# A two-layer graph attention kernel: its one-trip loop written out, and its opening loads and first projection in another order

## The chip, the cores and the metric

The kernel runs on one core of a Trainium2 chip. The core has five engines that each take their own stream of instructions in order: TensorE (PE, matrix products and transposes), VectorE (DVE), ScalarE (ACT), GpSimd (POOL) and SyncE (SP, which here only issues DMAs). They meet through semaphores. The metric is the device time of one launch in microseconds (us); lower is better.

## The reference

128 graphs of 128 nodes with 384 features go through two attention layers, each after a layer norm and a ReLU and with a residual. Both layers have 12 heads of 32; `adj` masks the first layer's scores and is added to the second's.

```python
h = jnp.maximum(_layernorm(x), 0.0)
q, k, v = split(h @ Wq + bq), split(h @ Wk + bk), split(h @ Wv + bv)      # layer 0
scores = einsum('bhqd,bhkd->bhqk', q, k) / sqrt(32) + beta * adj
scores = where(adj > 0, scores, -9e15)
x = x + einsum('bhqk,bhkd->bhqd', softmax(scores), v)
h = jnp.maximum(_layernorm(x), 0.0)
q, k, v = h @ Wq1.T, h @ Wk1.T, h @ Wv1.T + bv1                            # layer 1
a = softmax(einsum(q, k) * 384 ** -0.5 + adj)
x = x + einsum(a, v) @ Wo1.T + bo1
```

## The kernel before

**Units and phases.** Four graphs make a group, and a group in one layer is a *unit*; there are 64 units. A unit is normed (DVE, ACT, POOL), turned by a DMA transpose into `h`, projected on PE in ten *jobs* (0 to 5 make q and k by column blocks, 6 to 9 make the values of a graph each), and attended in twelve *chunks* of four heads (c = 0 to 11). These steps belong to different phases: a `Phase` (from line 130) attends one unit, projects the next, norms the one after that and finishes the tail of the one before. A phase has 12 slots, and every engine's code walks through slots and places within a slot and emits what is due. So the order on each engine is written by hand, in tables: `PROJ` says how many of a unit's 90 projection matmuls stand in each slot's three places, and the `..._AT` tables place the other steps.

**Products in two halves.** Every weight and every activation is split into two fp16 parts, high and low, and a product takes three matmuls (high by high, low by high, high by low). For a weight that is one ACT instruction (`high_weight`, w_hi, L658) and one DVE instruction (`low_weight`, w_lo, L766), both on a float32 copy that SP loads (`load_weight`, L457) into a buffer that is used for something else later (`staging`). `LOAD_SLOTS`, `HIGH_SLOTS` and `LOW_SLOTS` say in which slot of which of the first four phases each of the seven weights (0 to 6) is handled. Weights 0, 1 and 2 are layer 0's for q, k and v.

**q and k.** The result of a job is taken from its bank by ACT (`part_hi`, L679) and DVE (`part_lo`, L865); a bank is free for the job after next once `part_lo` is written. Three DMAs of 128 KB for each job (L483, L487) then copy the parts into `stack`, in which a head's 96 rows stand together. Scores for chunks 0, 1 and 2 wait for the stacks of jobs 0 and 1, 2 and 3, 4 and 5 (`stack_in`, one semaphore for each pair). The first job of a unit waits for all four of its DMA transposes (`h_in`, L518).

**The opening.** Phase 0 norms unit 0 and takes weights 0, 1 and 2 apart. Phase 1 projects unit 0 and norms unit 1, whose input is `x_second` (it stands in the buffer `probs_t`). The transposes of unit 0 read h_rows0, h_rows1, o_t and o_norm, in this order; so do those of unit 1. Phase 2 is the first that attends. All DMAs are issued by SP, on one queue. The two norm tables say in which slots the four graphs of a unit begin: `NORM_SLOTS_FIRST` is (0, 1, 2, 3).

**The loop.** `run_phases` (L211) writes seven phases, then a loop (`Fori`, L214) over `inside`, then twelve more. The loop's step is 24 pairs of phases and it makes one trip, so its body is all 48 phases, and the values it waits for are constants in the program as built; each engine has one jump into the body and one addition, comparison and branch at its end.

## Time and profile before

| what | us |
|---|---|
| median of three runs | 2213.1 (2212.03 to 2213.17) |
| the profiled execution, its own time | 2209.57 |
| its span, first instruction to last | 2207.8 |
| PE busy in the span | 2155.2 (98%) |
| ACT busy | 2048.4 (93%) |
| DVE busy | 1818.2 (82%) |
| POOL busy | 1511.8 (68%) |
| chain that ended last: PE's share of it | 82% |

The first line is what is to be predicted; the others come from one profiled execution. Busy time is the time in which an engine works on an instruction; what it waits for between is in the view of waits. The chain is followed back from the last instruction to whatever released each step.

### The profile page before, as it was taken

To read this page: it belongs to the slowest core of one execution; us is meant where nothing else is said; L and a number is where in the kernel's file an instruction comes from. 1 tells how busy PE (TensorE), PEld (TensorE's weight loads), DVE (VectorE), ACT (ScalarE), POOL (GpSimd) and SP (SyncE) were. 2 spreads that over 40 slices of the span, in tenths; PEclk is the share of its full clock that TensorE was granted. 3 is DMA by queue.
4 is the path that set the end of the run, shared out by engine and by line. 5 is a ranking of instruction groups with operands and counts; after the bars stand their busy time and mean duration, and the time that the engine had idled before them with its cause. 6 is when DMAs were issued, how large, how long until landed. Compare 5 with 4: busy or idle time off the path is not lost.

```text
span 2207.8 us, 69320 instructions
## 1 busy us (share of the span) xinstructions
PE 2155.2 (98%) x19968; PEld 1423.3 (64%) x19968; DVE 1818.2 (82%) x10202; ACT 2048.4 (93%) x7824; POOL 1511.8 (68%) x2407
## 2 busy tenths in 40 slices
PE   5999999999999999999999999999999999999997
PEld 2566666666666666666666666666666666666665
DVE  5888888888888888888888888888888888888787
ACT  4999999999999999999999999999999999999987
POOL 1567766767667767667676677676676776676675
PEclk9999999999999999999999999999999999999999
DMA  9886768778577787787797777776776876868852
GB/s 192 170 134 140 132 136 145 128 134 159 125 137 141 135 146 134 138 145 132 133 154 129 135 144 132 143 147 129 141 136 133 158 127 134 146 131 133 140 99 60
DMA packets 461307, 302.88 MB, mean 137 GB/s; under 512 B 228480, under 2 KB 460928, under 8 KB 460928
## 3 DMA queue, kind: packets, MB, share of 16 engines
q1 hardware_dynamic: 460928, 298.45, 73.8%
q8 instruction: 162, 2.65, 0.6%
q14 instruction: 217, 1.78, 0.4%
HBM read 71.83 MB, written 25.17 MB: 44 GB/s over the span
## 4 chain that ended last, share of the span: by engine, by line
PE 82%; ACT 6%; DVE 6%; issue 4%; DMA 1%; SPq 0%; DVEq 0%; POOL 0%; ACTq 0%
PE job_bank L999 43%; PE pt_bank L1022 13%; PE o_bank L1035 8%; PE score_bank L1012 7%; ACT probs L667 4%; PE inv_bank L1058 3%; PE post_bank L1068 2%; PE post_bank L1072 2%; PE post_bank L1069 2%; PE post_bank L1050 2%; DVE neg L787 1%; DVE part_lo L865 1%; ACT part_hi L679 1%; DVE inv_wide L857 1%; DMA x_norm<-in_x 1%
## 5 line engine op out<-in xcount | busy, mean ns | idle before, releaser
L667 ACT ACTIVATE probs<-neg,neg_max 128x128 f32<-128x128 f32 x3072 | 1189.7, 394 | 45.4 <-DVE neg_max L787 45.4
L999 PE MATMUL job_bank<-h,w_hi 128*128 128x512 f16 x2304 | 725.4, 380 | 23.1 <-DMA h<-o_norm 21.1
L667 ACT ACTIVATION_READ_ACCUMULATOR probs<-neg,neg_max 128x1 f32 x3072 | 595.0, 194 | 0.0
L692 ACT ACTIVATE probs_t<-pt_bank 128x512 f32<-128x512 f32 x768 | 450.3, 586 | 29.1 <-PE pt_bank L1022 26.4
L1022 PE MATMUL pt_bank<-ident,probs 128*128 128x128 f32 x3072 | 464.1, 274 | 11.5 <-ACT probs_t L692 11.1
L999 PE MATMUL job_bank<-h,w_lo 128*128 128x512 f16 x1152 | 438.3, 380 | 0.0
L1022 PEld LDWEIGHTS pt_bank<-ident,probs 128*128 128x128 f32 x3072 | 366.1, 141 | 96.1 <-issue 16.9
L999 PE MATMUL job_bank<-w_hi,h 128*128 128x384 f16 x1536 | 411.9, 326 | 0.2 <-DVE part_lo L865 0.2
L599 POOL TENSOR_TENSOR pair_sum<-neg 128x256 f32<-128x256 f32 x384 | 281.1, 732 | 189.2 <-DVE neg_max L787 174.6
L787 DVE CUSTOM_DVE_ANT_0 neg<-score_bank,adj 128x128 f32<-128x128 f32 x1536 | 352.5, 285 | 44.2 <-issue 40.6
L787 DVE CUSTOM_DVE_ANT_0 neg<-score_bank,bias 128x128 f32<-128x128 f32 x1536 | 354.3, 287 | 15.2 <-issue 15.0
L999 PEld LDWEIGHTS job_bank<-h,w_hi 128*128 128x128 f16 x2304 | 222.0, 98 | 211.3 <-issue 32.0
L1012 PEld LDWEIGHTS score_bank<-stack 96*128 96x128 f16 x3072 | 232.5, 97 | 126.4 <-DVE neg_max L787 6.3
L1012 PE MATMUL score_bank<-stack 96*128 96x128 f16 x3072 | 299.2, 219 | 5.3 <-DMA stack<-part_lo 5.3
L787 DVE DVE_READ_ACCUMULATOR2_ANT neg_max<- 128x1 f32 x3072 | 253.4, 82 | 0.1
L999 PE MATMUL job_bank<-w_lo,h 128*128 128x384 f16 x768 | 250.6, 326 | 0.0
L568 POOL TENSOR_TENSOR rstd<-shift_var,minus_half 128x1 f32<-128x1 f32 x256 | 144.5, 564 | 146.3 <-DVE shift_var L825 146.3
L590 POOL TENSOR_TENSOR h_rows<-h_rows 128x384 f16<-128x384 f32 x248 | 226.8, 915 | 20.7
L618 POOL TENSOR_TENSOR x_mid<-x_res,o_rows 128x384 f32<-128x384 f32 x128 | 128.0, 1000 | 138.7 <-issue 110.3
L1035 PE MATMUL o_bank<-probs_t,v 128*32 128x128 f32 x6144 | 220.8, 277 | 0.0
L870 DVE SCALAR_TENSOR_TENSOR part_lo<-job_bank,part_hi 128x512 f16<-128x512 f32 x192 | 132.5, 690 | 97.6 <-ACT part_hi L683 95.3
L605 POOL TENSOR_TENSOR four_sum<-pair_sum 128x128 f32<-128x128 f32 x384 | 176.2, 459 | 38.6 <-POOL pair_sum L599 0.4
(75 smaller groups left out, 3511.0 us busy)
## 6 DMA issues: line engine op xcount, KB each, us to landing
stack<-part_hi SPq DMA_DIRECT2D x768, 128.0 KB, 3.7
stack<-part_lo SPq DMA_DIRECT2D x384, 128.0 KB, 4.0
x_res<-in_x SPq DMA_DIRECT2D x32, 768.0 KB, 6.0
out_x<-result_rows SPq DMA_DIRECT2D x128, 192.0 KB, 3.3
x_norm<-in_x SPq DMA_DIRECT2D x30, 768.0 KB, 6.8
adj<-in_adj SPq DMA_DIRECT2D x64, 256.0 KB, 3.7
h<-h_rows SPq DMA_TRANSPOSE x252, 4.0
x_norm<-in_x SPq DMA_DIRECT2D x4, 192.0 KB, 4.2
```

Source lines behind the costliest of these rows:

```text
L568: pool.tensor_tensor(rstd[:, b:b + 1], shift_var[:, b, 1:2], minus_half[:, :], ALU.pow).then_inc(rstd_done, 1)
L590: pool.tensor_tensor(h_rows[b % 2][:, 1, :], h_rows32[:, :], h_rows[b % 2][:, 0, :], ALU.subtract).then_inc(h_rows_ready, 1)
L599: pool.tensor_tensor(pair_sum[:, :, :], neg[c % 2][:, :, 0:NODES // 2], neg[c % 2][:, :, NODES // 2:NODES], ALU.add).then_inc(pair_sum_don ...
L605: pool.tensor_tensor(four_sum[b % 2][:, first:first + HC, :], pair_sum[:, :, 0:NODES // 4], pair_sum[:, :, NODES // 4:NODES // 2], ALU.add ...
L667: last = act.activation(probs[c % 2][:, h, :], neg[c % 2][:, h, :], ACT.Exp, bias=neg_max[:, b, first + h:first + h + 1], scale=-1.0, accu ...
L692: act.activation(probs_t[b % 2][:, first:first + HC, :].rearrange("p h q -> p (h q)"), pt_bank[:, :], ACT.Copy).then_inc(probs_t_ready, 1)
L787: last = dve.tensor_tensor_reduce(out=neg[c % 2][:, h, :], in0=score_bank[c % 2][:, P * h:P * (h + 1)], in1=bias, scale=(-1.0 / SCORE0 if ...
L870: last = dve.scalar_tensor_tensor(part_lo[t][:, c, :], job_bank[j % 2][:, :], scale, part_hi[t][:, c, :], ALU.mult, ALU.subtract)
L999: last = pe.matmul(to, stationary, moving, start=(m == 0), stop=(m == MATMULS - 1))
L1012: last = pe.matmul(score_bank[c % 2][:, P * h:P * (h + 1)], q[0:3 * HEAD, c % KC, h, nodes], k[0:3 * HEAD, c % KC, h, nodes], start=True, ...
L1022: last = pe.transpose(pt_bank[:, P * h:P * (h + 1)], probs[c % 2][:, h, :], ident[:, :])
L1035: last = pe.matmul(o_bank[d:d + HEAD, f:f + P], v32[u.parity][:, b, HEAD * h:HEAD * (h + 1)], probs_t[b % 2][:, h, :], start=True, stop=True)
```

## The change

Six things are changed. (1) `loop_unit`, `TURN` and the `Fori` go; Python writes out all phases, and the tests for whether a number is known go with them. (2) SP loads all four graphs of unit 0 ahead of weight 0. (3) The load of weight 2 (the values' weight) moves from the end of the opening loads to behind the transposes of unit 0, and its two halves are made in phase 1; ACT makes the halves of weights 0 and 1 behind the norm of unit 0. (4) In phase 1 the projection has its 90 matmuls from slot 0 on, nine in each of ten slots, and the norm of unit 1 begins a slot later. (5) The loads of `x_second`, of the first `adj0`, of `x_norm` for unit 2 and of `x_res` for unit 0 all stand ahead of phase 1 on SP; before, the last two stood behind it. (6) The first stack of unit 0 waits for two weights, and that of unit 1 for three.

```diff
-PROJ_FIRST = ((0, 0, 0),) * 4 + ((4, 4, 3),) * 6 + ((4, 4, 4),) * 2
+PROJ_FIRST = ((3, 3, 3),) * 10 + ((0, 0, 0),) * 2
...
+NORM_SLOTS_SECOND = (1, 2, 3, 4)
...
-LOAD_SLOTS = ({}, {}, {0: 3, 3: 4, 6: 5, 9: 6}, {})
-HIGH_SLOTS = ({2: 0, 3: 1, 5: 2}, {}, {3: 3, 6: 4, 9: 5}, {0: 6})
-LOW_SLOTS = ({4: 0, 6: 1, 8: 2}, {}, {4: 3, 7: 4, 10: 5}, {1: 6})
+LOAD_SLOTS = ({7: 2}, {}, {0: 3, 3: 4, 6: 5, 9: 6}, {})
+HIGH_SLOTS = ({4: 0, 5: 1}, {1: 2}, {3: 3, 6: 4, 9: 5}, {0: 6})
+LOW_SLOTS = ({6: 0, 7: 1}, {2: 2}, {4: 3, 7: 4, 10: 5}, {1: 6})
...
     for p in before()[first:]:
         phase(p)
-    with eng.Fori(FIRST_LOOP, LAST_LOOP + 2 - TURN, TURN) as i:
-        for k in range(TURN):
-            for p in inside(i, k):
-                phase(p)
+    for i in range(FIRST_LOOP, LAST_LOOP + 1):
+        for p in inside(i):
+            phase(p)
...
-            load_first(0)
-            load_first(1)
...
+            for b in range(GROUP):
+                load_first(b)
             load_weight(0)
-            load_first(2)
-            load_first(3)
             load_weight(1)
...
-            load_weight(2)
...
-                if j == 0 and isinstance(u.n, int) and u.n == 0:
-
-                    sp.wait_ge(w_lo_ready, 3)
+                if j == 0 and u.n < 2:
+
+                    sp.wait_ge(w_lo_ready, 2 + u.n)
...
-                    if p.weights == 0 and s == 5:
-                        sp.dma_start(x_second, x_groups[1]).then_inc(x_second_in, 16)
...
             phase(before()[0])
+            sp.dma_start(x_second, x_groups[1]).then_inc(x_second_in, 16)
             sp.dma_start(adj0[:, :, :], adj_groups[0]).then_inc(adj0_in, 16)
+            sp.wait_ge(centred_ready, GROUP)
+            sp.dma_start(x_norm[:, :, :], x_groups[2]).then_inc(x_norm_in, 16)
+            sp.dma_start(x_res[:, :, :], x_groups[0]).then_inc(x_res_in, 16)
             phase(before()[1])
-            sp.dma_start(x_res[:, :, :], x_groups[0]).then_inc(x_res_in, 16)
```

Three places of the order show it. The first is SP's queue in phase 0, from the last of the small loads on: before,

```order
L470 DMA bo_rows<-in_L1_gnn_bo 128x384
L457 DMA stack01<-in_L0_gnn_Wv 128x3x384
L518 DMA_TRANSPOSE h0<-h_rows0 128x6x128 [waits h_rows_ready]
L518 DMA_TRANSPOSE h0<-h_rows1 128x6x128 [waits h_rows_ready]
L518 DMA_TRANSPOSE h0<-o_t 128x6x128 [waits h_rows_ready]
L541 DMA probs_t1<-in_x 128x4x384
L518 DMA_TRANSPOSE h0<-o_norm 128x6x128 [waits h_rows_ready]
L546 DMA adj0<-in_adj 128x4x128
```

and in the changed kernel:

```order
L453 DMA bo_rows<-in_L1_gnn_bo 128x384
L500 DMA_TRANSPOSE h0<-h_rows0 128x6x128 [waits h_rows_ready]
L500 DMA_TRANSPOSE h0<-h_rows1 128x6x128 [waits h_rows_ready]
L500 DMA_TRANSPOSE h0<-o_t 128x6x128 [waits h_rows_ready]
L500 DMA_TRANSPOSE h0<-o_norm 128x6x128 [waits h_rows_ready]
L440 DMA stack01<-in_L0_gnn_Wv 128x3x384
L522 DMA probs_t1<-in_x 128x4x384
L523 DMA adj0<-in_adj 128x4x128
L525 DMA x_norm<-in_x 128x4x384 [waits centred_ready]
L526 DMA x_res<-in_x 128x4x384
L465 DMA stack00<-part_hi0 32x4x512 [waits part_hi_ready,w_lo_ready]
```

The four transposes of unit 0 have nothing large right ahead of them now, and five loads stand between them and the first stack. The second place is the end of phase 1 on SP (`stack00` and `stack10` are unit 0's q and k, h1 is unit 1's): before,

```order
L483 DMA stack10<-part_hi1 32x4x512 [waits part_hi_ready]
L483 DMA stack10<-part_hi1 32x4x512
L487 DMA stack10<-part_lo1 32x4x512 [waits part_lo_ready]
L536 DMA x_norm<-in_x 128x4x384 [waits centred_ready]
L548 DMA x_res<-in_x 128x4x384
L496 DMA adj0<-in_adj 128x4x128 [waits bias_ready]
```

and now:

```order
L500 DMA_TRANSPOSE h1<-o_t 128x6x128 [waits h_rows_ready]
L465 DMA stack10<-part_hi1 32x4x512 [waits part_hi_ready]
L465 DMA stack10<-part_hi1 32x4x512
L469 DMA stack10<-part_lo1 32x4x512 [waits part_lo_ready]
L500 DMA_TRANSPOSE h1<-o_norm 128x6x128 [waits h_rows_ready]
L478 DMA adj0<-in_adj 128x4x128 [waits bias_ready]
```

The last transpose of unit 1 stood ahead of the stacks of jobs 2 to 5; now it stands behind all 18 stacks of unit 0. The third place is PE where phase 1 passes into phase 2, the same rows in both kernels but for their lines; here the changed kernel's:

```order
L991 MATMUL score_bank1<-stack10,stack00 128x128 [waits stack_in10]
L991 MATMUL score_bank1<-stack10,stack00 128x128 x3
L978 MATMUL job_bank0<-h1,w_hi0 128x512 [waits v_ready,h_in1,h_in0]
L978 MATMUL job_bank0<-h1,w_hi0 128x512
L991 MATMUL score_bank0<-stack10,stack00 128x128 [waits neg_ready,stack_in20]
L991 MATMUL score_bank0<-stack10,stack00 128x128 x3
```

Behind the scores of chunk 1 stand two matmuls of unit 1's first job, which wait for its transposes, and then the scores of chunk 2, which wait for the last stacks.

## Rows read from the trace of the kernel before

**Rows 1.** The page, part 1: busy time of each engine, share, instructions.

```profile
PE 2155.2 (98%) x19968; PEld 1423.3 (64%) x19968; DVE 1818.2 (82%) x10202; ACT 2048.4 (93%) x7824; POOL 1511.8 (68%) x2407
```

**Rows 2.** Stretches of 67.27: length, busy time of each engine, PEclk, DMA.

```profile
217.27:284.54 67.27, 67.02 (x626) 44.37 (x624) 56.33 (x319) 63.53 (x246) 47.52 (x76) 1.00 0.75 140
...
351.81:419.08 67.27, 66.67 (x623) 44.09 (x622) 55.93 (x317) 63.26 (x244) 47.82 (x76) 1.00 0.82 139
...
1831.00:1898.30 67.30, 67.07 (x626) 44.47 (x625) 56.28 (x318) 63.61 (x245) 47.61 (x77) 1.00 0.75 139
```

**Rows 3.** PE's waits in 0 to 56: for whom, total, times, longest.

```profile
PE job_bank L999 <- DMA h<-o_norm: 21.1, 1, 21.1
PE score_bank L1012 <- DMA stack<-part_lo: 5.3, 1, 5.3
```

**Rows 4.** PE's waits in 54 to 2160.

```profile
PE inv_bank L1058 <- DVE inv_wide L857: 7.3, 29, 0.6
PE pt_bank L1022 <- ACT probs_t L692: 4.0, 10, 0.7
```

**Rows 5.** Timeline of SP, 0 to 29: start, length, what it issued.

```profile
2.12 0.96 SPq L452 DMA_DIRECT2D x_norm<-in_x  x2
...
7.18 0.43 SPq L457 DMA_DIRECT2D stack<-in_L_gnn_Wv  x1
9.11 3.86 SPq L518 DMA_TRANSPOSE h<-h_rows  x2
13.08 1.84 SPq L518 DMA_TRANSPOSE h<-o_t  x1
14.97 0.57 SPq L541 DMA_DIRECT2D probs_t<-in_x  x1
15.66 1.22 SPq L518 DMA_TRANSPOSE h<-o_norm  x1
...
26.25 1.22 SPq L518 DMA_TRANSPOSE h<-o_t  x1
```

**Rows 6.** The chain of waits, 0 to 60: start, length, what.

```profile
2.12 5.77 DMA x_norm<-in_x
```

**Rows 7.** DMAs issued in 40.5 to 43: KB each, us from issue to landing.

```profile
x_norm<-in_x SPq DMA_DIRECT2D x1, 768.0 KB, 10.0
x_res<-in_x SPq DMA_DIRECT2D x1, 768.0 KB, 11.5
x_mid<-in_L_gnn_Wq SPq DMA_DIRECT2D x1, 576.0 KB, 12.6
```

**Rows 8.** The stack tiles in 27 to 49: issues, and shortest, median, longest landing.

```profile
L483 SPq DMA_DIRECT2D stack<-part_hi x12: 584/602/706, 27.6 to 39.3; - x12
...
L487 SPq DMA_DIRECT2D stack<-part_lo x6: 593/600/602, 29.0 to 40.0; - x6
...
DMA to landing us min/median/max: 3.1/5.1/8.7
```

**Rows 9.** DMAs issued in 22 to 27.

```profile
h<-o_t SPq DMA_TRANSPOSE x1, 2.7
```

**Rows 10.** Stretches of the opening: columns as in Rows 2.

```profile
21.10:26.60 5.50, 5.50 (x14) 1.87 (x15) 4.38 (x23) 4.42 (x8) 2.54 (x4) 1.00 0.30 52
26.60:43.40 16.80, 16.09 (x88) 7.95 (x86) 9.29 (x25) 5.74 (x14) 0.00 (x0) 1.00 1.07 147
43.40:48.70 5.30, 0.02 (x1) 0.00 (x0) 0.81 (x8) 1.87 (x10) 0.00 (x0) 0.86 1.13 184
48.70:53.90 5.20, 5.19 (x23) 3.58 (x24) 3.14 (x24) 1.97 (x7) 1.18 (x3) 0.50 1.08 356
...
52.60:113.40 60.80, 57.13 (x524) 36.64 (x523) 49.88 (x269) 60.05 (x222) 33.99 (x50) 0.99 0.87 171
```

**Rows 11.** Timeline of PE and ACT behind the wait for the stacks.

```profile
48.71 0.61 PE L1012 MATMUL score_bank<-stack 96*128 96x128 f16 x4 [5.29 <-DMA stack<-part_lo]
...
54.58 0.67 ACT L679 ACTIVATE part_hi<-job_bank,b_cols 128x512 f16<-128x512 f32 x1
```

More of the change, by code:

```diff
@@ L167, in before @@
         Phase(norm=u(0), weights=0, norm_slots=NORM_SLOTS_FIRST),
-        Phase(project=u(0), norm=u(1), look=u(0), bias=0, weights=1, table=PROJ_FIRST, norm_slots=NORM_SLOTS_FIRST),
+        Phase(project=u(0), norm=u(1), look=u(0), bias=0, weights=1, table=PROJ_FIRST, norm_slots=NORM_SLOTS_SECOND),
         Phase(attend=u(0), project=u(1), norm=u(2), look=u(1), bias=1, weights=2),
@@ L222, in some @@
 def some(value):
-    return not isinstance(value, int) or value > 0
+    return value > 0
 def unit_of_chunk(p, s):
@@ L250, in layer1_unit @@
 def layer1_unit(group, off):
-    if not isinstance(group, int):
-        return group * 2 + (2 * off + 2)
     return next(n for n in range(UNITS) if layer_and_group(n) == (1, group + off))
 def shared(u):
-    return isinstance(u.n, int) and u.n < SHARED_UNITS
+    return u.n < SHARED_UNITS
 def chunk(u, c):
@@ L364, in turned_before @@
         def turned_before(u, b):
-            if isinstance(u.n, int) and u.n < SHARED_UNITS:
+            if u.n < SHARED_UNITS:
                 return u.n * 32
@@ L373, in normed_rows @@
                 return x_mid[:, b, :]
-            return x_second[:, b, :] if isinstance(u.n, int) and u.n == 1 else x_norm[:, b, :]
+            return x_second[:, b, :] if u.n == 1 else x_norm[:, b, :]
         consts_in = sem("consts_in")
@@ L610, in add_rows @@
                 pool.wait_ge(o_rows_ready, u.group * GROUP + (b + 1))
-                if isinstance(u.n, int) and u.n == 0:
+                if u.n == 0:
                     pool.wait_ge(w_lo_ready, 4)
@@ L710, in centre @@
                 act.wait_ge(shift_ready, n + 1)
-                if isinstance(u.n, int) and u.n < SHARED_UNITS:
+                if u.n < SHARED_UNITS:
                     if u.n > 0:
```

52 lines of the change are left out of this document (19 added, 33 removed).

## The prediction

> **What bounds the kernel now.** I read the page's first part, then the kernel in stretches as long as a pair of phases, then who waits in the first 56 us, and last the DMAs there.
>
> PE is busy for 98% of the span [rows 1]. A pair of phases takes 67.27 us. PE works 67.02 us of it in the pair at whose start the loop's body is entered, and 67.07 of 67.30 in the pair in which the loop ends (it ends near 1833) [rows 2]. A pair that was disturbed lost 0.36 more (66.67). So the middle of the kernel is PE's own work, and neither end of the loop shows in it.
>
> What PE does not work is 52.6 us in all (2207.8 - 2155.2). Half of it is in the opening: 21.1 us until the last of unit 0's transposes, `h<-o_norm`, has landed, and 5.3 us until the last stack of unit 0 has (from 43.4 to 48.7) [rows 3]. In 54 to 2160, nearly the whole kernel, the two largest waits are 7.3 and 4.0 us [rows 4]. Nothing in the change touches the rest, at the end.
>
> **The loop (1).** Removed are one jump, one addition and one compare-and-branch for each engine; the waits in the body held constants already. Of these PE shows nothing [rows 2], so I take 0. The bounds are the disturbed pair's: a gain of 0.4 us if such a loss went, a loss of 0.4 if one more pair had it. The page "Runtime: NRT & Kernel Launch" of the Trainium skill, section "Instruction fetch mechanics", says that a taken branch to a page outside the fetched window makes the sequencer wait for the fetch, and prefers full unrolling; by it something would be gained at the entry. The trace doesn't agree, since the pair that begins there lost no more than the next ones.
>
> **The first projection starts earlier (2, 3).** Before, graphs 2 and 3 of unit 0 were issued behind weight 0, and the first of them landed 5.8 us after its issue [rows 6]; weight 2 was issued at 7.18, ahead of the transposes; and SP took 3.86 us for the first two transposes and 1.84 for the third, where an undisturbed one takes 1.22 [rows 5]. The norm of unit 0 also waited on ACT and DVE for halves of weights. Now SP reaches the transposes at about 7.2. Four of them take SP 4 x 1.22 = 4.9 us at best, and 3.86 + 1.84 + 1.22 = 6.9 us if they are as slow as before, so SP is through with them between 12.1 and 14.1; I take 13.1. The last is then issued at 11.9 and lands 2.7 us later at the least [rows 9] and some 3.3 with others ahead of it: 15.0 instead of about 21.0. PE starts **6 us earlier**.
>
> This does not reach the end by itself. From its start to its stop at 43.4 PE took 5.5 + 16.8 = 22.3 us [rows 10]. With 2 us more for the norm of unit 1, which now stands among the q and k parts on ACT and DVE, it is through by about 39, and there it waits again.
>
> **What it then waits for (4, 5).** The queue of DMAs decides, and it is served in the order of issue. The 18 stacks were issued from 27.6 to 40.0; the first landed 3.1 us after its issue, at 30.7, and the last 8.7 us after its, at 48.7 [rows 8]. Between lie 17 further stacks and one transpose: 18.0 us for 18 items, 1.0 us for each. The loads behind them: `x_norm` landed at 50.6, `x_res` at 52.8, and `adj0` and a weight together at 55.2 (issued at 40.64, 41.28 and 42.62) [rows 7]. So 768 KB take 2.1 us, and 256 and 576 KB together 2.4.
>
> Now five loads stand ahead of the stacks: weight 2 and `adj0` 2.4 us, and `x_second`, `x_norm`, `x_res` 3 x 2.1 = 6.4 (unrounded), in all 8.8. They can start when the transposes have landed at 15.0, with some 0.4 to get going: they end at 24.2. By then stacks have been issued for 4 us (job 0 is through on PE at about 19), so the queue doesn't run dry. Behind them stand 18 stacks and now all four transposes of unit 1, 22 items at 1.0: **the last lands at 46.2**. It is `h<-o_norm` of unit 1, for which PE's first job of that unit waits. SP issues it at about 37, so that the issue has more than 5 us of cover; if that cover were gone, each us of delay would cost a us.
>
> Of the 6 us, 2.1 + 2.1 are thus given back by moving `x_norm` and `x_res` ahead of the stacks.
>
> **From there to the end.** PE fell to the lower of its two clocks, 1.2 GHz, in the wait and stood at 0.50 from 48.7 to 53.9 [rows 10]; it now idles 7 us instead of 5.3, so the same comes again. Before, ACT took `part_hi` at 54.58, 5.9 us after PE went on [rows 11], when PE's first job of unit 1 was just through. Now two matmuls of that job (0.4 us each at that clock: 14 in 5.5 us [rows 10]) come behind the wait instead of ahead of it, so that `part_hi` comes at 46.2 + 5.9 + 0.8 = 52.9; a few matmuls of it run at full clock already, which takes off 0.5: 52.3. That is **2.3 us earlier** than 54.6. Two waits fall away beside it: DVE's for `x_norm` (landed at 50.6, two us behind the last stack) and with it ACT's; but PE is later than they are, so they only count where PE's order is faster than I think. From 52.6 to 113.4 ACT is busy 60.05 of 60.80 us [rows 10] with the same instructions in both kernels, so it keeps the 2.3 us, no more and no less; and behind that the order is the same.
>
> Sum: loop 0, opening -2.3. The profiled execution's own time would go from 2209.57 to 2207.3. It lies 3.5 below the median of the runs, 2213.1; the forecast for the median is **2210.8**.
>
> The two ends of this sum: with SP through at 12.1, loads at once behind the last transpose at 13.6 and items at 0.9 us, the last lands at 13.6 + 8.8 + 19.8 = 42.2, 6.3 us less. With SP through at 14.1, the last transpose at 16.4, 0.8 to get going and items at 1.0, it is 16.4 + 0.8 + 8.8 + 22.0 = 48.0, and the gain is 0.5.
>
> **Rivals.**
>
> A. *The queue is faster than 1.0 us for each item.* Transposes are counted at a stack's price, and the loads may overlap with them. At 0.9, and the rest as in the forecast, 24.2 + 19.8 = 44.0: 4.5 us gained, 2208.6. For it: ACT and DVE no longer wait for `x_norm`. Against it: the row's own 18.0 us for 18 items. A page goes much further: "DMA: Bandwidth & Descriptors" of the Trainium skill, section "Where 436 GB/s comes from", gives about 435 GB/s as the ceiling for copies within SBUF, by which a stack of 128 KB would take an estimated 0.3 us and there would be no second wait. The trace doesn't agree: 1.0 us for each.
>
> B. *No net gain.* The moved loads cost all that the earlier start brings: if the first transposes land as late behind the small loads as at 16.4 and the loads run into the stacks with another 0.5, the last item lands at 48.5, and the time is 2213.1. For it: the queue had little idle time to give: its share was 0.30 in 21.1 to 26.6, some 3.9 us free, but 1.07 and 1.13 from there to 48.7 [rows 10], against 4.2 us of new load. Against it: weight 2 and `x_second` no longer stand between the transposes, where SP's issues were slow [rows 5].
>
> C. *Slower: the code written out meets the fetch of instructions at worse places.* The pair in 351.81 to 419.08 lost 0.36 us [rows 2], in DVE's chain to `inv_wide`, for which PE waits in nearly every pair already (29 times, 0.25 each [rows 4]). Instructions are shifted by one to four places on each engine. If this made such a loss recur in all 28 pairs, it is 28 x 0.36 = 10.1 us: 2213.1 - 2.3 + 10.1 = 2220.9. It decides from 7 pairs on, where it eats the gain. Against it: the pairs within the body and behind it have the same time, though they lie differently in the code.
>
> D. *The change doesn't do what it says*: PE's earlier start is lost at once, since the parts of q and k on DVE stand behind the stats of `x_second` (lands at about 20) and are not ready for the queue. They have 4 us of cover; the time would be that of B.
>
> **How the numbers follow.** The forecast (gain 1 to 4) has 0.58, A (4 to 6) 0.17, B with D (no gain to 1) 0.18, C 0.07. What a measurement of this kernel can tell from no change is about 0.2%, 4.4 us: faster is below 2208.7, slower above 2217.5. Faster gets A and a little of the forecast's edge, 0.20; slower gets C, 0.06; the same gets 0.74. For 8 in 10 the range takes in the forecast, most of A and B, with some tenths for the scatter of the runs: 2206.8 to 2213.6.
>
> **What would show it.** In the trace of the changed kernel: PE's first wait ends at 14 to 16.5 instead of 21.1. Its second, now for `h<-o_norm` of unit 1 and not for a stack, begins near 38 and ends at 45 to 47.5. The clock falls in it and stays at 0.50 for 5 us behind it. `part_hi` of unit 1 comes at 51.5 to 53.5. Pairs take 67.27 throughout. I would be wrong if the last transpose landed before 44 (A), if PE didn't fall to the low clock (2.6 us more gained), or if pairs took another time (C).

## The result

| | median us | range | runs |
|---|---|---|---|
| before | 2211.74 | 2210.45 to 2213.76 | 18 |
| changed | 2207.62 | 2205.84 to 2209.29 | 18 |

The ratio is 0.9981, with a 95% interval of 0.9974 to 0.9988: the change saves 4.1 us. I had forecast 2.3 us. The median lies inside the range of the forecast, 2206.8 to 2213.6, its direction is right, and its size is not. Of the 3.2 us between the time forecast (2210.8) and the one measured, 1.4 belong to the starting value: the three runs that I had of the kernel before had a median of 2213.1, and 18 runs have 2211.7. The gain itself accounts for 1.8.

The page of the changed kernel, part 1, answers to [rows 1]:

```profile
span 2204.1 us, 69307 instructions
...
PE 2154.9 (98%) x19968; PEld 1422.6 (65%) x19968; DVE 1817.4 (82%) x10202; ACT 2048.2 (93%) x7824; POOL 1511.2 (69%) x2407
```

The engines do the same work as before; the span is 3.7 us shorter (2207.8 - 2204.1). So the gain is waiting that went. The same stretches as in [rows 2], taken 5.09 us earlier, from length and busy times to PEclk, DMA share and GB/s:

```profile
212.18:279.45 67.27, 67.04 (x626) 44.40 (x624) 56.34 (x319) 63.53 (x246) 47.53 (x76) 1.00 0.76 141
346.72:413.99 67.27, 67.02 (x626) 44.36 (x625) 56.29 (x319) 63.55 (x246) 47.55 (x76) 1.00 0.77 139
1825.91:1893.21 67.30, 67.07 (x626) 44.48 (x625) 56.30 (x318) 63.61 (x245) 47.61 (x77) 1.00 0.75 139
```

Shifted by 5.09 us, every engine does the same in them to a few hundredths, 1614 us apart: nothing is gained or lost between 212 and 1893 us. The second one was disturbed before (66.67 of PE work) and isn't now, but the next one is (66.68), and the waits of PE in 50 to 2155 amount to the same as in [rows 4] (`inv_bank` 7.6 us in 30 waits, before 7.3 in 29). All of the gain is made in the opening. PE's waits in 0 to 50, with for whom, total, times, longest, answer to [rows 3]:

```profile
PE job_bank L978 <- DMA h<-o_norm: 14.9, 1, 14.9
PE job_bank L978 <- issue: 6.4, 1, 6.4
PE job_bank L978 <- DVE part_lo L844: 1.8, 4, 0.9
```

The first wait ends at 14.95 instead of 21.1. The second stands between phase 1 and unit 1's first job. PE's timeline there and ACT's first `part_hi` of unit 1 answer to [rows 11]:

```profile
43.91 1.01 PE L978 MATMUL job_bank<-h,w_hi 128*128 128x512 f16 x2 [6.43 <-issue]
...
49.53 0.69 ACT L658 ACTIVATE part_hi<-job_bank,b_cols 128x512 f16<-128x512 f32 x1 [0.23 <-PE job_bank L978]
```

`part_hi` comes at 49.53 and not at 54.58, 5.05 us earlier. The wait carries the label "issue", which means that the profile found no releaser. The DMAs issued in 36 to 38 name it: columns are KB each and us from issue to landing.

```profile
stack<-part_lo SPq DMA_DIRECT2D x1, 128.0 KB, 7.2
h<-o_norm SPq DMA_TRANSPOSE x1, 7.2
```

SP issued `h<-o_norm` at 36.59 (below), so it landed at 43.8, and PE went on at 43.91. The first and the last stack were issued at 19.23 and 35.87 and landed at 26.0 and 43.1. The 18 stacks' shortest, median and longest time from issue to landing answers to [rows 8]:

```profile
DMA to landing us min/median/max: 5.9/6.6/7.5
```

No stack landed as soon after its issue as the first one of before (3.1): the queue had work ahead of it throughout.

The opening in stretches answers to [rows 10]. PE's clock is at the lower level (0.50, that is 1.2 of 2.4 GHz) behind the second wait, as forecast:

```profile
21.10:37.40 16.30, 14.79 (x80) 7.22 (x80) 12.44 (x38) 7.42 (x12) 2.19 (x4) 1.00 1.18 213
37.40:43.90 6.50, 0.08 (x2) 0.02 (x1) 2.40 (x20) 3.19 (x16) 0.00 (x0) 0.82 1.27 162
43.90:48.40 4.50, 4.49 (x19) 2.72 (x20) 1.61 (x17) 1.74 (x6) 1.05 (x3) 0.50 0.45 143
48.70:108.30 59.60, 56.21 (x523) 36.05 (x522) 49.32 (x265) 58.62 (x217) 32.65 (x47) 1.00 0.88 166
```

SP's timeline answers to [rows 5], start and length of each issue:

```profile
7.48 3.15 SPq L500 DMA_TRANSPOSE h<-h_rows  x2
10.73 1.22 SPq L500 DMA_TRANSPOSE h<-o_t  x1
12.06 1.22 SPq L500 DMA_TRANSPOSE h<-o_norm  x1
13.34 0.57 SPq L440 DMA_DIRECT2D stack<-in_L_gnn_Wv  x1
...
15.05 0.92 SPq L525 DMA_DIRECT2D x_norm<-in_x  x1
16.00 0.54 SPq L526 DMA_DIRECT2D x_res<-in_x  x1
19.23 1.34 SPq L465 DMA_DIRECT2D stack<-part_hi  x2
...
36.59 1.85 SPq L500 DMA_TRANSPOSE h<-o_norm  x1
```

**In the profiled executions the opening gained 5.1 us and the span 3.7; the median of the runs gained 4.1.** What lies between the first two is near the end. 0.3 us went in a wait for `inv_wide` at 2117.5 that the kernel before didn't have. Then, in the profiled run of the changed kernel, the clock fell once more while PE did its last nine matmuls; in that of before it didn't. The stretches, PE's busy time first behind the length, PEclk third from the end, of the changed kernel:

```profile
2198.38:2201.10 2.72, 2.71 (x9) 1.05 (x9) 0.00 (x0) 0.00 (x0) 0.84 (x1) 0.57 0.00 0
```

and of the kernel before:

```profile
2203.19:2204.80 1.61, 1.61 (x9) 0.75 (x9) 0.00 (x0) 0.00 (x0) 0.85 (x1) 1.00 0.00 0
```

The same nine matmuls take 2.72 us instead of 1.61, and 1.1 us is lost. It belongs to the execution, not to the change: of the 14 executions that were profiled for this document, 11 have the last nine matmuls at 2.1 to 3.0 us, `loop_only` among them, whose program is the kernel before but for the loop; before, `w2_early` and `late_loads` have them at 1.6. In six of the 14 the clock also fell some 42 us before the end, and PE came out 1.4 to 1.7 us later. `loop_only` is one of them; here it is and then the kernel before, in the same stretch counted from the end:

```profile
2164.00:2179.00 15.00, 11.70 (x122) 8.57 (x121) 11.24 (x71) 12.55 (x54) 7.58 (x13) 0.89 0.22 67
2160.80:2175.80 15.00, 11.45 (x131) 8.36 (x129) 11.34 (x68) 13.94 (x58) 8.80 (x15) 1.00 0.31 89
```

The span of `loop_only` is 2211.0 instead of 2207.8, and most of the difference is these two places: 1.5 us and 1.1. So the profiled execution of before is one in which the clock fell in neither, and where single executions are compared below, it is in the opening. How often the clock falls there in the runs without a profile isn't shown, and so neither is why the median gained 1.0 us less than the opening.

### The profile page after: what moved, and what is told of

It is laid out like the page before. It is cut to its first block, busy times and chain, and to the rows that moved or that the text cites. A ratio compares the mean times of both kernels' runs of the same rounds, so it can differ in the third digit from the quotient of the medians.

```text
span 2204.1 us, 69307 instructions
## 1 busy us (share of the span) xinstructions
PE 2154.9 (98%) x19968; PEld 1422.6 (65%) x19968; DVE 1817.4 (82%) x10202; ACT 2048.2 (93%) x7824; POOL 1511.2 (69%) x2407
## 4 chain that ended last, share of the span: by engine, by line
PE 82%; ACT 6%; DVE 6%; issue 4%; SPq 1%; DMA 1%; DVEq 0%; ACTq 0%
PE job_bank L978 43%; PE pt_bank L1001 13%; PE o_bank L1014 8%; PE score_bank L991 7%; ACT probs L646 4%; PE inv_bank L1037 3%; PE post_bank L1047 2%; PE post_bank L1051 2%; PE post_bank L1048 2%; PE post_bank L1029 2%; DVE part_lo L844 1%; DVE neg L766 1%; ACT part_hi L658 1%; DVE inv_wide L836 1%; DVE off_zero L827 1%
## 5 line engine op out<-in xcount | busy, mean ns | idle before, releaser
L978 PE MATMUL job_bank<-h,w_hi 128*128 128x512 f16 x2304 | 724.4, 380 | 24.5 <-DMA h<-o_norm 14.9
L766 DVE CUSTOM_DVE_ANT_0 neg<-score_bank,bias 128x128 f32<-128x128 f32 x1536 | 354.1, 286 | 20.8 <-issue 20.5
L584 POOL TENSOR_TENSOR four_sum<-pair_sum 128x128 f32<-128x128 f32 x384 | 176.4, 459 | 38.3
```

Source lines behind the costliest of these rows:

```text
L584: pool.tensor_tensor(four_sum[b % 2][:, first:first + HC, :], pair_sum[:, :, 0:NODES // 4], pair_sum[:, :, NODES // 4:NODES // 2], ALU.add ...
L766: last = dve.tensor_tensor_reduce(out=neg[c % 2][:, h, :], in0=score_bank[c % 2][:, P * h:P * (h + 1)], in1=bias, scale=(-1.0 / SCORE0 if ...
L978: last = pe.matmul(to, stationary, moving, start=(m == 0), stop=(m == MATMULS - 1))
```

## The experiments

Each run's ratio is to the kernel before, run beside it on the same chip (its medians were 2211.9, 2211.5 and 2210.9 in the three groups); it comes from the runs one by one and can differ from the quotient of the medians in the last digit or two. The changed kernel was not run in these groups; its own ratio is 0.9981 (0.9974 to 0.9988). "Last lands" is the landing of `h<-o_norm` of unit 1. In `loop_only` and `proj_back`, as before, it isn't the last item of the queue: stacks stand behind it, and the last of them landed at 49.0 and 50.3.

| run | median us | ratio, 95% interval | last lands | `part_hi` of unit 1 |
|---|---|---|---|---|
| `loop_only` | 2211.41 | 1.0001 (0.9992 to 1.0010) | 36.2 (before 35.9) | 54.88 |
| `proj_back` | 2210.97 | 0.9999 (0.9990 to 1.0008) | 38.3 | 54.26 |
| `table_only` | 2212.15 | 1.0007 (0.9998 to 1.0016) | 49.0 | 55.55 |
| `x_order_back` | 2206.87 | 0.9978 (0.9969 to 0.9987) | 43.4 | 49.37 |
| `w2_early` | 2207.62 | 0.9982 (0.9973 to 0.9992) | 45.7 | 51.32 |
| `late_loads` | 2205.71 | 0.9974 (0.9964 to 0.9985) | 42.9 | 49.05 |
| `late_xres` | 2204.86 | 0.9970 (0.9959 to 0.9981) | 43.2 | 49.31 |
| `turns_last` | 2204.96 | 0.9969 (0.9957 to 0.9981) | 42.3 | 47.73 |
| `turns_and_loads_last` | 2206.05 | 0.9977 (0.9968 to 0.9986) | 41.6 | 48.84 |
| `turns_and_xres_last` | 2204.67 | 0.9970 (0.9958 to 0.9982) | 41.5 | 46.86 |
| `warm_gap` | 2206.74 | 0.9981 (0.9972 to 0.9990) | 43.4 | 47.80 |

The two right-hand columns come from one execution each. They are not the same thing as the medians, and `late_xres`, profiled twice below, shows by how much an execution can differ.

### The loop alone

```diff
-    with eng.Fori(FIRST_LOOP, LAST_LOOP + 2 - TURN, TURN) as i:
-        for k in range(TURN):
-            for p in inside(i, k):
-                phase(p)
+    for k in range(TURN):
+        for p in inside(FIRST_LOOP, k):
+            phase(p)
```

> The kernel before with only the loop written out: the same 48 phases, one jump, one addition and one compare-and-branch less on each engine, nothing else moved. Theory 1 (the loop costs nothing, all of the gain is in the opening): the time of before within 0.5 us, pairs of phases at 67.27 us, unit 1 begins its exponentials at 81.7 as before. Rival (a part of the 4.1 us comes from the code without jumps): at least 1 us less than before, and pairs that were disturbed (67.63 once) no longer so.

Measured: 2211.41 us, ratio 1.0001. The pairs at the loop's entry and end, same stretches as [rows 2]:

```profile
217.27:284.54 67.27, 67.04 (x626) 44.38 (x625) 56.34 (x321) 63.55 (x245) 47.65 (x77) 1.00 0.75 140
1831.00:1898.30 67.30, 67.07 (x627) 44.51 (x626) 56.34 (x319) 63.58 (x244) 47.60 (x77) 1.00 0.76 138
```

A loop of one trip costs nothing that can be seen within the interval, some 2 us either way, and rival C has nothing to stand on: in `loop_only` and in the changed kernel the pairs of phases keep their time. The section "Instruction fetch mechanics" of the page "Runtime: NRT & Kernel Launch" in the Trainium skill has a taken branch to a page that isn't fetched stall the sequencer. No row here shows such a stall at the entry, nor a gain where the branch is gone.

### The two halves of the reordering

`proj_back` is the changed kernel with the old table and the old slots for the norm of unit 1.

```diff
-PROJ_FIRST = ((3, 3, 3),) * 10 + ((0, 0, 0),) * 2
+PROJ_FIRST = ((0, 0, 0),) * 4 + ((4, 4, 3),) * 6 + ((4, 4, 4),) * 2
...
-        Phase(project=u(0), ..., norm_slots=NORM_SLOTS_SECOND),
+        Phase(project=u(0), ..., norm_slots=NORM_SLOTS_FIRST),
```

> The changed kernel with the old table for the first projection and the old slots for unit 1's norm; the loads and weights stay changed. What differs is where the norm of unit 1 and its transposes stand: three transposes ahead of all stacks, one behind the sixth. Theory 1 (the wait before unit 1's first job ends with the last item of the queue): here the wait is for the last stack again. If the norm of unit 1 waits for x_second (19.8) before the parts of q and k are made, the stacks begin 5 us later than in the changed kernel, near 24.5 to 25, and at 1.0 us apart end near 45; then the time is 1 to 1.5 above the changed kernel. Rival (the table does nothing, the loads all): the time of the changed kernel within 0.5.

Measured: ratio 0.9999, the whole gain is gone. PE's waits in 0 to 56:

```profile
PE job_bank L978 <- DMA h<-o_norm: 15.3, 1, 15.3
PE job_bank L978 <- DVE part_lo L844: 10.3, 2, 10.1
PE score_bank L991 <- DMA stack<-part_lo: 2.5, 1, 2.5
```

PE starts at 15.3, nearly as in the changed kernel, does two jobs and then waits 10.1 us for the first `part_lo`. DVE's timeline says why; the bracket is the idle time ahead and its releaser:

```profile
20.25 0.56 DVE L792 BATCH_NORM_STATS2 stats<-probs_t 128x6 f32<-128x384 f32 x1 [6.93 <-DMA probs_t<-in_x]
...
29.86 1.41 DVE L844 SCALAR_TENSOR_TENSOR part_lo<-job_bank,b_cols,part_hi 128x512 f16<-128x512 f32 x2 [1.66 <-ACT part_hi L658]
```

By the old slots the norm of unit 1 stands ahead of the first parts on DVE, and it waits for `x_second` until 20.25. ACT makes its first `part_hi` only at 29.16, behind its part of the norm of all four graphs, and DVE's part comes at 29.86. PE's two banks are full until then. The start that came 6 us earlier is lost in the next wait. I had expected the stacks to begin near 24.5 and the time to be 1 to 1.5 us above the changed kernel; they began at 29.93, and the loss is the whole gain.

`table_only` is the other half: the kernel before, with the new table and slots alone.

```diff
-PROJ_FIRST = ((0, 0, 0),) * 4 + ((4, 4, 3),) * 6 + ((4, 4, 4),) * 2
+PROJ_FIRST = ((3, 3, 3),) * 10 + ((0, 0, 0),) * 2
...
+NORM_SLOTS_SECOND = (1, 2, 3, 4)
...
-... table=PROJ_FIRST, norm_slots=NORM_SLOTS_FIRST),
+... table=PROJ_FIRST, norm_slots=NORM_SLOTS_SECOND),
```

> The kernel before with part 4 alone: nine projection matmuls in each of ten slots of phase 1 from slot 0 on, and the norm of unit 1 a slot later. Loads, halves of weights, loop and the place of x_norm and x_res as before. Theory (the table only pays where the transposes of unit 0 land earlier): PE still starts at 21.1 and needs its 22.3 us, so it is through with phase 1 near 43.5 as before. What changes is its second wait: unit 1's last transpose now stands behind all stacks. The first stack is issued 2.5 us or so earlier than at 27.6, 22 items at 0.85 each from about 28.3 end at 47: that is 1.7 before the last stack of before (48.7), so a gain of 1 at most, time 2210.5 to 2211.5. Rival (the table carries the gain by itself, since without it the other parts gave ratio 0.9999): 4 us less than before, 2207.5.

Measured: ratio 1.0007, no gain. PE's waits in 0 to 56:

```profile
PE job_bank L1000 <- DMA h<-o_norm: 20.5, 1, 20.5
PE job_bank L1000 <- issue: 7.2, 1, 7.2
```

PE starts at 20.5 and waits from 41.98 on for the last transpose, which lands at 49.0. The last stack of before landed at 48.7, so the opening is no shorter; and since the job's first matmuls now stand behind this wait, `part_hi` comes at 55.55, 0.7 to 1.0 us later than in the two kernels with the old order (54.88 and 54.58). I had expected a gain of up to 1 us from a last landing at 47: the first stack was issued at 25.3 as thought, but from its landing at 28.4 to the last one at 49.0 an item took 0.98 on the mean, and not 0.85.

**Each half alone brings nothing, both together bring 4 us.** The earlier transposes of unit 0 are of use only if the parts of q and k are made early too, and the parts can be made early only if the transposes are.

### Two parts whose undoing the medians don't show

`x_order_back` takes graphs 2 and 3 of unit 0 behind weight 0 again; `w2_early` loads weight 2 ahead of unit 0's transposes again (its halves stay in phase 1).

```diff
-            for b in range(GROUP):
-                load_first(b)
+            load_first(0)
+            load_first(1)
             load_weight(0)
+            load_first(2)
+            load_first(3)
```

> The changed kernel with graphs 2 and 3 of unit 0 loaded behind weight 0 again. Theory 1: they land 3 us later (near 8), the norm of unit 0 ends 2 us later, PE starts near 16.5 to 17 instead of 14.95; the loads behind the transposes shift by as much, the last transpose of unit 1 lands 1.5 to 2 us later, and the time is 1.5 to 2 above the changed kernel. Rival (the transposes wait for the small loads ahead of them on the queue anyway, so the norm has room): PE starts at 15 to 15.5 and the time is that of the changed kernel within 0.5.

```diff
-LOAD_SLOTS = ({7: 2}, {}, {0: 3, 3: 4, 6: 5, 9: 6}, {})
+LOAD_SLOTS = ({}, {}, {0: 3, 3: 4, 6: 5, 9: 6}, {})
...
             sp.dma_start(bo_rows[:, :], b1o.partition_broadcast(P)).then_inc(consts_in, 16)
+            load_weight(2)
```

> The changed kernel with the load of weight 2 back at the end of the opening loads, ahead of unit 0's transposes. Theory 1 (the queue is served in order): the transposes of unit 0 land 1.5 to 2 us later, PE starts near 17, but the loads behind them are shorter by the same 576 KB, so that x_res lands at 25.5 as before and the last transpose of unit 1 at 44; the time is that of the changed kernel within 0.5. Rival (PE's earlier start is what brought the gain): 1.5 to 2 us above the changed kernel.

Measured: ratios 0.9978 and 0.9982, both the changed kernel's within their intervals, which leave some 2 us open either way. With the old order of the x loads PE started at 15.7 instead of 14.95, but the last transpose landed at 43.4, 0.4 earlier than in the changed kernel: the first stacks landed 0.6 apart there and not 0.7, and so the queue made good for the later start. I had expected it 1.5 to 2 us later; the rival, the same time, fits.

With weight 2 early, PE's first wait ended at 18.1, 3.2 us later than in the changed kernel, and the last transpose landed at 45.7, 1.9 us later. The median, 2207.62, fits my expectation (within 0.5 of the changed kernel), but the trace doesn't fit its reason: I had put the landing of `x_res` at 25.5 and the last one at 44, and `x_res` landed at 27.1, since SP reached the loads only behind the later transposes (`x_second` at 16.5 instead of 14.0). So of the 3.2 us by which PE starts earlier, 1.9 reached the end of the opening in these two executions. Whether the whole time keeps them isn't shown: the medians say no difference, and can't tell 1.9 us from none.

### What the moved loads and the transposes cost

`late_loads` puts `x_norm` and `x_res` behind phase 1 again, `late_xres` only `x_res`.

```diff
-            sp.wait_ge(centred_ready, GROUP)
-            sp.dma_start(x_norm[:, :, :], x_groups[2]).then_inc(x_norm_in, 16)
-            sp.dma_start(x_res[:, :, :], x_groups[0]).then_inc(x_res_in, 16)
             phase(before()[1])
+            sp.wait_ge(centred_ready, GROUP)
+            sp.dma_start(x_norm[:, :, :], x_groups[2]).then_inc(x_norm_in, 16)
+            sp.dma_start(x_res[:, :, :], x_groups[0]).then_inc(x_res_in, 16)
```

> The changed kernel with the loads of x_norm (unit 2) and x_res (unit 0) back behind phase 1 on SP. Theory 1 (the queue of DMAs is served in order, and these two loads, which took from 20.6 to 25.3 in the changed kernel's trace, stand in the way of the stacks and of the last transpose): the last transpose of unit 1 lands at 39.5 instead of 43.8, PE waits 2 us instead of 6.4 and keeps its high clock, the first part_hi of unit 1 comes at 44.5 instead of 49.5, and the time is 5 us below the changed kernel, 9 below before. Rival (the issue of stacks or the norm of unit 1 is nearly as late as the queue, so that little is won, or DVE's wait for the later x_norm takes its place): the last transpose lands after 42, 0 to 2 us below the changed kernel.

> The changed kernel with only x_res behind phase 1; x_norm stays ahead of the stacks. In the changed kernel nine stacks ran 0.66 apart right behind a load; with both loads moved (the run before) the queue ran dry and they ran 0.89 apart, which ate the 4.7 us. Theory 3 (a stack's pace is 0.66 when it stands right behind plain loads, 0.9 to 1.0 behind a pause or a transpose): the first stack lands at 23.5, the ninth at 29, the last transpose at 41.3, 2.5 earlier than in the changed kernel, and the time is 2 to 2.5 below it. Rival (the end is set by something else than the queue's backlog at the start, such as the cycle of one transpose and three stacks that takes 3.8 us): the last transpose lands at 42.9 to 43.5 as in the two other runs, and the time is within 1 us of the changed kernel.

`turns_last` leaves the loads where the change put them and issues unit 1's four transposes together, behind all 18 stacks.

```diff
+            def turns(u, b):
+                if u is None or u.n == 1 and b < GROUP - 1:
+                    return []
+                return [(u, k) for k in range(GROUP)] if u.n == 1 else [(u, b)]
...
-                        if u is not None:
+                        for u, b in turns(u, b):
```

> The changed kernel with the four transposes of unit 1 issued together behind all 18 stacks of unit 0 instead of one behind each of jobs 2 to 5. In the changed kernel's trace the nine stacks ahead of the first transpose landed 0.66 us apart, and those behind it 1.0. Theory 2 (a transpose among the stacks slows the copies behind it): all 18 land 0.66 apart, the last stack at 25.3 + 12 = 37.3 or as soon as it is issued, some 38.5; the last transpose then at 43, bound by SP's issues. Rival (the pace falls with something else, such as how far the loads ahead have left the 16 engines apart, or what the other engines do): the stacks fall to 1.0 apart after some nine of them all the same, the last stack lands at 41 or later and the last transpose at 44 to 45.

Measured: 2205.71, 2204.86 and 2204.96 us. By the ratios they are 1.5, 2.4 and 2.7 us faster than the changed kernel, but the intervals overlap with its own (0.9974 to 0.9988), so none of the three is shown to be faster. I had expected 5 us from `late_loads` and a last transpose at 39.5, and from `late_xres` one at 41.3; they landed at 42.9 and 43.2. In `late_loads` 4.7 us of loads left the queue ahead of the stacks (they had landed from 20.6 to 25.3), and the last transpose landed only 0.9 us earlier. The first stack was issued only at 19.9 and found the queue nearly empty, and so it landed 3.0 us earlier and not 4.7, at 23.0. From there on the first eight stacks landed 0.88 apart, not 0.6 to 0.7 as in the changed kernel, and the ninth was only 0.9 us ahead. In `turns_last` all 18 landed 0.57 apart on average. Its stack tiles in 18 to 44 (number, ns of an issue, first and last start), then the landings:

```profile
L465 SPq DMA_DIRECT2D stack<-part_hi x12: 547/598/700, 21.6 to 33.5; - x12
...
L469 SPq DMA_DIRECT2D stack<-part_lo x6: 547/601/622, 22.9 to 34.1; - x6
...
DMA to landing us min/median/max: 3.1/4.6/5.9
```

The first landed 5.9 us after its issue at 21.56, at 27.4, the last 3.1 after 34.12, at 37.2: 9.8 us for 17. In [rows 8] the landing took longer from one to the next (3.1 to 8.7); here it takes less and less: the queue catches up with SP. The last transpose, issued at 39.6 behind the other three, landed at 42.3, so that at the end SP's issues bound this kernel, as expected.

From these I drew a theory: the stacks are quick right behind a backlog of plain loads, and slow where the queue had run dry. Two runs were to test it.

```diff
 (turns_and_loads_last: turns_last, and)
+            phase(before()[1])
             sp.wait_ge(centred_ready, GROUP)
             sp.dma_start(x_norm[:, :, :], x_groups[2]).then_inc(x_norm_in, 16)
             sp.dma_start(x_res[:, :, :], x_groups[0]).then_inc(x_res_in, 16)
-            phase(before()[1])
 (turns_and_xres_last: turns_last, and)
             sp.wait_ge(centred_ready, GROUP)
             sp.dma_start(x_norm[:, :, :], x_groups[2]).then_inc(x_norm_in, 16)
+            phase(before()[1])
             sp.dma_start(x_res[:, :, :], x_groups[0]).then_inc(x_res_in, 16)
-            phase(before()[1])
```

> The changed kernel with the transposes of unit 1 behind all stacks, and x_norm and x_res behind these: neither a transpose nor a plain load is near the stacks. Theory 2 (only transposes among the stacks slow them): 0.65 apart, or as issued. Theory 3 (they are fast only right behind plain loads that have left the queue with work): 0.85 to 0.9 apart from the first at 23 on, the last at 38 to 38.5. In both cases the last transpose lands near 42, bound by SP's issues, and the time is that of the kernel with the transposes last within 0.7.

> The changed kernel with unit 1's four transposes behind all 18 stacks, and x_res for unit 0 loaded behind phase 1. Theory (the stacks take 0.65 each only right behind a backlog of plain loads, 0.88 each where the queue had run dry): with x_norm alone ahead, the first two or three stacks are quick and the rest 0.88 apart, so the last stack lands at 37.5 to 38, and the last transpose at 41 to 41.6. PE's second wait ends near 41.5, a gain of 2.3 over the changed kernel's 43.8; time 2204.5 to 2205.5, the same as either edit alone (2204.96 and 2204.86). Rival (the two edits save independent work): 2.7 and 2.8 add up, time near 2202.2.

`turns_and_loads_last` landed as the theory said: the first eight stacks 0.89 apart, the last at 37.5, the last transpose at 41.6. Its median, 2206.05, was 1.1 us above that of `turns_last` and not within 0.7. `turns_and_xres_last` did not: I had put the stacks 0.88 apart, since `late_xres` had them so with the same loads ahead, and the first seven landed 0.53 to 0.65 apart. The median, 2204.67, came out as expected all the same, and the rival (2202.2, the two edits add up) fell. It is the fastest median of all, but not apart from `late_xres` and `turns_last`.

So `late_xres` was profiled once more.

> The same kernel as late_xres, profiled once more (the changed kernel with x_res for unit 0 loaded behind phase 1). In late_xres the third to ninth stack landed 0.89 apart; in turns_and_xres_last, which issues the same instructions on SP up to 26.6 us, they landed 0.56 apart. Theory 4 (the pace of the stacks changes from one execution to the next, whatever the order): here they may land 0.55 to 0.66 apart. Rival (the pace belongs to the program, by something that the order on SP doesn't show): 0.89 apart again, within 0.02. A single repeat that shows 0.89 doesn't rule theory 4 out; one that shows 0.66 or less rules the rival out.

Measured: 2204.45 us in its one run beside 2212.0 of before, and 0.59 to 0.65 apart for the first eight stacks, where the same kernel had 0.89 from the third on. From the third stack to the eighth it is 3.0 us (24.9 to 27.9); in `late_xres` it was 4.4 (25.1 to 29.5). The last transpose landed at 41.3 instead of 43.2, and `part_hi` of unit 1 came at 47.58 instead of 49.31. **The same stacks of the same kernel were served at two paces in two executions**, and the opening moved by 1.7 us, 0.4 of it by an earlier start of PE (14.9 instead of 15.3).

The two traces differ in one more thing ahead of the change of pace: when the fourth stack was issued. Here are ACT's second `part_hi`, the issue of the fourth stack, and its time to landing, in `late_xres`:

```profile
22.32 0.69 ACT L658 ACTIVATE part_hi<-job_bank,b_cols 128x512 f16<-128x512 f32 x1 [1.16 <-PE job_bank L978]
23.03 0.55 SPq L465 DMA_DIRECT2D stack<-part_hi  x1
stack<-part_hi SPq DMA_DIRECT2D x1, 128.0 KB, 2.9
```

and in the repeat:

```profile
21.35 0.69 ACT L658 ACTIVATE part_hi<-job_bank,b_cols 128x512 f16<-128x512 f32 x1 [0.61 <-PE job_bank L978]
22.06 0.55 SPq L465 DMA_DIRECT2D stack<-part_hi  x1
stack<-part_hi SPq DMA_DIRECT2D x1, 128.0 KB, 3.5
```

PE's first matmuls took 0.43 us each until 21.2 in `late_xres` and until some 19.8 in the repeat, and 0.21 from there on (the granted clock stands at 1.00 throughout in both), so in `late_xres` PE was through with its second job 1.0 us later, and the fourth stack came 1.0 us later. It landed after 2.9 us, as soon as a stack does that finds nothing ahead (3.1 for the first one in six kernels). So the queue may have just run dry there, and the 0.89 behind it would be the pace of a queue that ran dry once more. That is argued and not shown, and one trace speaks against it: in `turns_and_xres_last` the fifth to the seventh stack landed 3.1 to 2.8 us after their issue and stayed 0.53 to 0.56 apart. The two profiles are also from two chips. What decides the pace stays open.

What is left of the theory is a count. In six kernels no load stood in the way of the first stack, and it landed 3.1 us after its issue (before, `loop_only`, `proj_back`, `table_only`, `late_loads`, `turns_and_loads_last`); there the first six landed 0.86 to 0.89 apart on the mean, without exception. In the eight profiles with a load of 768 KB right ahead of them it was 0.58 to 0.70 in seven, and 0.77 in `late_xres`, which went to 0.89 from the fourth stack on.

### What the low clock costs

`warm_gap` is the changed kernel with 26 matmuls more on PE, in its second wait.

```diff
                 if j == 0 and m == 0:
+                    if u.n == 1:
+                        pe.wait_ge(v_ready, 3)
+                        for _ in range(26):
+                            pe.matmul(job_bank[0][:, :], w_hi[0][:, 0, 0:P], h[0][:, 0, 0, :], start=True, stop=True)
                     pe.wait_ge(h_in[0], u.n * 32 + 32)
```

> The changed kernel with 26 matmuls more: in PE's second wait (37.5 to 43.9), ahead of the wait for unit 1's transposes, it multiplies weight 0's high half by unit 0's h into job bank 0, 512 columns each; the first real matmul of the job overwrites it. About 5.6 us of work in a wait of 6.4. Theory (the low clock is what the idle time brings, and costs half of the 4.5 us in which PE worked at 0.50): the granted clock stays at 1.00 through 37 to 50, part_hi of unit 1 comes 2.2 earlier than 49.5, and the time is 2205.4. Rival 1 (the low stretch comes anyway, only elsewhere): no gain, 2207.6. Rival 2 (ACT or the transposes bound the stretch behind 43.9 in any case): the clock stays up, but part_hi comes at 48.5 or later and the time is 2206.8 or more.

Measured: 2206.74 us, ratio 0.9981, the changed kernel's. The stretches of its wait and behind it:

```profile
37.40:43.90 6.50, 6.50 (x38) 3.16 (x36) 2.74 (x20) 3.19 (x16) 0.00 (x0) 1.00 1.28 175
43.90:48.40 4.50, 4.50 (x35) 2.97 (x34) 2.69 (x23) 3.26 (x12) 2.38 (x5) 1.00 0.33 111
```

The clock stays at 1.00, and PE does 35 matmuls in the 4.5 us in which it did 19 at 0.50. `part_hi` of unit 1 comes 1.7 us earlier (47.80), where I had expected 2.2. Of these, 0.4 are not the clock's: the last transpose landed at 43.4 instead of 43.8, and PE went on at 43.49 instead of 43.91. From there to `part_hi` it is 4.3 us instead of 5.6, so that the low clock costs 1.3. The gain doesn't last: unit 1's first softmax step, 76.70 in the changed kernel, comes at 74.96. But that of unit 2 comes at 109.06, against 109.36: 1.4 of the 1.7 us are given back. ACT's waits in 50 to 113 show where:

```profile
ACT probs L646 <- DVE neg_max L766: 1.5, 3, 1.0
ACT w_hi L637 <- DMA result_rows<-in_L_gnn_Wo: 1.3, 1, 1.3
```

The second row, 1.3 us, isn't there in the changed kernel. ACT takes weight 6 apart in phase 2, and its load was issued at 69.53 and took 9.1 us (78.7), with the stacks ahead of it landing 1.0 us apart again:

```profile
result_rows<-in_L_gnn_Wo SPq DMA_DIRECT2D x1, 576.0 KB, 9.1
```

In `turns_last` and `turns_and_xres_last`, which reach unit 1 as early (74.88 and 74.02), there is no such wait, and the gain is kept; in `turns_last` the same load landed at 75.9. In the changed kernel it landed at 78.1, 1.0 us before ACT came to it; before, 0.4. So the low clock does cost the opening 1.3 us, and whether an opening that is faster still keeps its gain depends on the load of weight 6, that is on the queue once more. Neither rival had named it. The time I had expected, 2205.4, didn't come.

## Why the prediction was right or wrong

- **Loop 0, the middle 0.** Right: `loop_only` has ratio 1.0001, and the pairs take 67.27 us in both kernels. Rival C fell.
- **PE starts at 15.0 instead of 21.** Right: 14.95. SP was through with the transposes at 13.3, forecast 13.1.
- **PE is through with phase 1 near 39 and waits again.** Right, though early: the wait began at 37.5. The 2 us that I added for the norm of unit 1 between the parts were mostly not lost: PE waited 1.8 us for DVE's `part_lo`, but the stretch of 22.3 us was done in 22.5.
- **The loads end at 24.2.** 1.1 us too early: `x_res` was issued at 16.0 and landed 9.3 later, at 25.3. From the last transpose's landing at 14.8 the five loads took 10.5 us, and I had 0.4 and 8.8.
- **22 items at 1.0 us each, last landing 46.2.** This is the step that failed, by its size. From 25.3 to 43.8 it is 18.5 us for 22 items, 0.84 each. The first nine took 6.1 us instead of 9, the other 13 took 12.4 instead of 13. The 18.0 us for 18 items of [rows 8] held two paces, which I had averaged: 0.9 for the first, behind a queue that had run dry, and 1.0 for the rest. The new kernel has neither. Its first nine stacks, behind the loads, landed 5.5 us apart from first to ninth, 0.69 each; then a transpose and three stacks came every 3.8 us, 0.95 each. The error is 3.5 us, and with the loads' 1.1 the other way the last item lands 2.4 us earlier than forecast. Rival A, which I gave 0.17, has the number that came, 44.0 against 43.8; by the sign that I had set for it (a last transpose before 44) the forecast of the queue was wrong and A was right. Why the first stacks landed faster behind the loads stays open, as said above.
- **The clock falls in the wait and costs as much as before.** It fell, at 0.50 until 48.4, which is 4.5 us of PE's work and not 5.2. This and the matmuls behind it put `part_hi` 5.7 us behind the landing, where I had 6.2 (5.9 + 0.8 - 0.5; the 52.3 is 52.4, if the terms are added as written). The 0.4 us for each of the two matmuls came from a row with PEclk at 1.00, where the matmuls took that long all the same; at 0.50 the two took 1.0 together. `warm_gap` prices the low clock at 1.3 us; my "2.6 us more gained" without it was too high, and would not have reached the end.
- **ACT keeps the gain.** Right: `part_hi` 5.05 earlier, unit 1's first softmax step 5.04 (76.70 against 81.74), the pairs 5.09.
- **The sum.** -2.3 became -5.1 in the opening: -3.5 for the items, +1.1 for the loads, -0.4 behind them. Near the end, which I had taken as untouched, the profiled run lost 0.3 in one more wait and 1.1 by the clock, which leaves 3.7. The median gained 4.1.
- **Rivals B and D.** The loads did not eat the gain (B), and the parts came early enough (D). But D's mechanism is real: `proj_back` shows it at full size. What keeps it away is the norm that begins a slot later, a part of the change to which I had given no price of its own.
- **The chances.** A gain of 4.1 us lies just within the bound of 0.2% (0.19%), the case to which I gave 0.74. It lies in the class of rival A (4 to 6, 0.17) and not in that of the forecast (1 to 4, 0.58). That the time lies in the range is in part luck. The range was set around a starting value that was 1.4 us too high; had all of the opening's 5.1 us come off the median of 2211.7, the time would be 2206.6, below the range.

What stays open is what sets the pace of the stacks in the queue, and so which of `late_xres`, `turns_last` and `turns_and_xres_last` is best. By the ratios to before, all three are some 2.4 to 2.7 us faster than the changed kernel (0.9970 and 0.9969 against 0.9981), but the intervals overlap.

## What to carry to other kernels

An average pace of a queue is no price for an item in another order: before using it, look at whether the queue had run dry or was backed up in each part of the stretch, and carry both paces as the bounds. A start that comes earlier is worth only what the next wait leaves of it, and two moves that are worth nothing alone can be worth the whole together, so undo each in turn rather than price it by itself. When an opening has become faster, look for the load that is needed next (here weight 6), since it may have been in time by a few tenths of a us only.

## What the runs showed of the hardware

- Copies of 128 KB within the core's memory took 0.5 to 1.0 us each in the same queue, by the mean distance of their landings, and one kernel (`late_xres`) showed 0.6 in one profile and 0.89 in another for the same stacks. The Trainium skill, page "DMA: Bandwidth & Descriptors", section "Where 436 GB/s comes from", puts copies within SBUF at about 435 GB/s, by which one would take an estimated 0.3 us; no stretch of stacks came near it. The figure is for all 16 ports together, and these copies write 32 of the 128 partitions (`32x4x512`); no run here changes that number, so it isn't shown whether that is the reason.
- With transposes between the stacks, three stacks and one transpose took 3.8 us, from one transpose's landing to the next, in the changed kernel, `late_loads` and `x_order_back` alike.
- The granted clock of TensorE fell at the end of 11 of 14 profiled executions, behind a wait of 1.9 us for `o_hi`, and made the last nine matmuls 2.1 to 3.0 us long instead of 1.6; in the other three, which have the same wait, it didn't. In six it also fell some 42 us before the end, at a cost of 1.4 to 1.7 us. Both are a part of the scatter of some 3.4 us between the runs of one kernel.
